# A gated delta net with an FP4 feed-forward layer on one core: every engine meets the steps of an element in another order

## The reference

```python
xn = layernorm(x)
x = x + delta_net(xn) + fp4_ffn(xn)

# delta_net: 12 heads, keys of 64, values of 128
q, k, v = (silu(causal_conv4(xn @ W)) for W in (Wq, Wk, Wv))
q, k = l2norm(q) * 64 ** -0.5, l2norm(k)
g, beta = -exp(A_log) * softplus(xn @ Wgk + dt_bias), sigmoid(xn @ Wb + b_b)
for t in range(256):                       # per head, S is 64 x 128
    S = S * exp(g[t])
    S = S + outer(k[t], (v[t] - k[t] @ S) * beta[t])
    o[t] = q[t] @ S
o = o * rsqrt(mean(o * o) + 1e-5) * g_norm_weight * silu(xn @ Wg)
out = o @ Wo

# fp4_ffn: inputs, weights and the 352 hidden values are rounded
# to FP4 in blocks of 16 along the last axis
h = silu(quant(xn) @ quant(w_gate).T) * (quant(xn) @ quant(w_up).T)
out = quant(h) @ quant(w_down).T
```

## Time and profile before

| | |
|---|---|
| median of 3 runs | 2864.97 us |
| lowest, highest | 2863.22, 2868.68 us |
| the profiled execution | 2873.21 us |
| its span | 2871.5 us |
| instructions | 73819 |
| mean granted clock of TensorE | 0.984 |
| busy: PE, DVE, ACT, POOL | 92%, 84%, 80%, 57% |

### The profile page before, as it was taken

How to read it: one execution, slowest core, us unless ns; L and a number is a source line. 1 busy time by engine, 2 the same in 40 slices (tenths; PEclk the granted TensorE clock), 3 DMA queues, 4 the chain that set the end, 5 groups by cost and what they waited for, 6 DMA issues and landing times.

```text
span 2871.5 us, 73819 instructions
## 1 busy us (share of the span) xinstructions
PE 2652.8 (92%) x25679; PEld 2086.6 (73%) x25679; DVE 2419.4 (84%) x6817; ACT 2289.1 (80%) x7010; POOL 1634.4 (57%) x2418
## 2 busy tenths in 40 slices
...
PEclk8899999999999999999999999999999999999997
...
GB/s 69 22 37 20 30 37 33 31 36 16 36 37 32 32 30 21 36 37 30 34 28 24 35 37 26 37 26 24 37 37 26 37 18 32 37 37 26 36 14 24
DMA packets 319326, 90.30 MB, mean 31 GB/s; under 512 B 283056, under 2 KB 310000, under 8 KB 318960
## 3 DMA queue, kind: packets, MB, share of 16 engines
...
...
## 4 chain that ended last, share of the span: by engine, by line
PE 45%; DVE 27%; POOL 13%; issue 6%; DMA 4%; ACT 3%; SPq 2%; DVEq 0%; POOLq 0%; ACTq 0%
DVE UP L982 7%; POOL laneT L587 5%; POOL laneA L590 5%; DVE vc L887 5%; DVE KQ L887 5%; PE bank_o L1308 4%; PE ring L1142 4%; PE ring L1200 4%; PE bank_e L1278 3%; PE ring L1167 3%; PE ring L1343 3%; PE bank_e L1290 3%; PE bank_e L1294 2%; PE bank_e L1285 2%; PE ring L1108 2%
## 5 line engine op out<-in xcount | busy, mean ns | idle before, releaser
L590 POOL TENSOR_TENSOR laneA<-laneA,laneT 96x30 f32<-96x30 f32 (+14 forms) x960 | 513.1, 534 | 75.2
L587 POOL TENSOR_TENSOR laneT<-laneA 96x30 f32<-96x30 f32 (+14 forms) x960 | 516.9, 538 | 68.0
L887 DVE SCALAR_TENSOR_TENSOR KQ<-ring,ckq,KQ 128x255 f32<-128x255 f32 (+2 forms) x1152 | 459.6, 472 | 10.2 <-ACT KQ L672 4.4
L887 DVE SCALAR_TENSOR_TENSOR vc<-ring,cvv,vc 128x255 f32<-128x255 f32 (+2 forms) x1152 | 461.8, 470 | 0.0
L1027 DVE SCALAR_TENSOR_TENSOR V<-bank_o,eG,V 128x128 f32<-128x128 f32 x384 | 133.4, 347 | 284.5 <-PE bank_o L1314 203.1
L982 DVE SCALAR_TENSOR_TENSOR UP<-ring,cj,gm 128x256 f32<-128x256 f32 x768 | 315.4, 476 | 22.4 <-PE ring L1167 19.7
L575 POOL TENSOR_TENSOR sqk<-sse,phalf 128x8 f32<-128x8 f32 x96 | 157.4, 1640 | 250.3 <-DVE sse L957 250.3
L569 POOL TENSOR_TENSOR gm<-g,mle 128x512 f32<-128x512 f32 x192 | 197.5, 1051 | 175.8 <-DVE UP L982 165.7
L751 ACT ACTIVATE eps<-bank_e 128x128 f32<-128x128 f32 x384 | 106.2, 276 | 219.8 <-PE bank_e L1294 182.8
L582 POOL MEMSET laneA<- 96x32 f32 x32 | 4.9, 154 | 473.8 <-DMA laneA<-to_lanes 473.8
L600 POOL TENSOR_TENSOR rO<-ov,mhalf 128x8 f32<-128x8 f32 x96 | 166.4, 1733 | 155.9 <-DVE ov L1038 155.4
...
## 6 DMA issues: line engine op xcount, KB each, us to landing
to_lanes<-UP SPq DMA_DIRECT2D x128, 96.0 KB, 2.7
...
UP<-from_lanes SPq DMA_DIRECT2D x128, 96.0 KB, 3.1
...
xin<-_attn_hidden_states_dram SPq DMA_DIRECT2D x32, 128.0 KB, 3.6
xres<-_attn_hidden_states_dram SPq DMA_DIRECT2D x32, 128.0 KB, 2.2
```

Source lines behind the costliest of these rows:

```text
L587: link(nc.gpsimd.tensor_tensor(t, A[:, 0:m, j:j + 1].broadcast_to([LANES, m, n]), A[:, j:j + 1, j + 1:BLK].broadcast_to([LANES, m, n]), AL ...
L590: link(nc.gpsimd.tensor_tensor(w, w, t, ALU.add))
L887: ins = nc.vector.scalar_tensor_tensor(acc[:, n, s:T], src[:, n * T:n * T + T - s], wt(n)[:, TAPS - 1 - s:TAPS - s], acc[:, n, s:T], ALU.m ...
```

## The change

The table `ORDER` is replaced by another with the same steps. Besides, an unused table `KEEP` and blank lines go, so a line after stands 23 lower than the same line before (L558 becomes L535, L903 L880, L1308 L1285). The count of the instructions of each kind is the same. Some steps change their offset, that is, they go over the iteration's border: `LANEP 6` and `7`, `STORE` and `XR` from 1 to 0 (the same work, done in the next iteration), and `VPs 4` too. Around the places of the next section the diff reads, cut:

```diff
 ORDER = (
-    ("QK", 0, 1), ("VPs", 5, 0), ("ZB", 0, 1), ("QKr", 0, 1), ("ZBr", 0, 1), ("QKt", 0, 1), ("QK", 1, 1),
-    ("QN", 5, 1), ("MZ2r", 0, 0), ("LN", 0, 2), ("SE", 3, 0), ("GRr", 4, 1), ("SSr", 2, 1), ("XQ0", 0, 1),
-    ("FU", 0, 1), ("LOUT", 0, 1), ("SQ", 8, 0), ("FUr", 0, 1), ("SE", 9, 0), ("LLOAD", 0, 1), ("FUm", 0, 1),
+    ("VPs", 4, 0), ("VPs", 5, 0), ("QK", 0, 1), ("ZB", 0, 1), ("ZBr", 0, 1), ("QK", 1, 1), ("QKr", 0, 1),
+    ("VT", 5, 0), ("QKt", 0, 1), ("KW", 0, 0), ("VT", 2, 0), ("QK", 2, 1), ("LANEP", 6, 0), ("ZBe", 0, 1),
+    ("LANEP", 7, 0), ("QK", 3, 1), ("ZBg", 0, 1), ("GC", 0, 1), ("QKr", 1, 1), ("VTr", 2, 0), ("QK", 4, 1),
+    ("SE", 8, 0), ("GRr", 11, 1), ("MZ2r", 2, 0), ("SO", 8, 0), ("LOUT", 0, 1), ("SQ", 8, 0), ("GP", 0, 0),
+    ("LLOAD", 0, 1), ("SE", 9, 0), ("VPt", 3, 1), ("SQ", 9, 0), ("SO", 9, 0), ("FU", 0, 1), ("FUr", 0, 1),
+    ("LN", 0, 2), ("SQ", 10, 0), ("SE", 10, 0), ("SO", 10, 0), ("GPr", 0, 0), ("FUm", 0, 1), ("LANEP", 0, 1),
```

More of the change, by code:

```diff
@@ L25 @@
 TURNED = 3
-KEEP = ((("CJ", 2, 1), ("KTr", 0, 1)), (("CJ", 2, 1), ("OS", 0, 1)), (("KW", 0, 0), ("SO", 5, 0)), (("KW", 1, 0), ("SO", 5, 0)), (("KW", 2, 0), ("SO", 5, 0)), (("KW", 3, 0), ("SO", 5, 0)), (("ZBr", 0, 1), ("XQ0", 0, 1)), (("ZB", 0, 1), ("QK", 2, 1)), (("ZBr", 0, 1), ("QKt", 2, 1)), (("QK", 2, 1), ("FU", 0, 1)), (("GPr", 0, 0), ("OG", 0, 0)), (("GPr", 1, 0), ("OG", 1, 0)), (("GPr", 2, 0), ("OG", 2, 0)), (("GPr", 3, 0), ("OG", 3, 0)), (("GPr", 4, 0), ("OG", 4, 0)), (("GPr", 5, 0), ("OG", 5, 0)))
 WEIGHTS_AT = ("FU", 0)
@@ L73 @@
-    ("CJ", 2, 1), ("GRr", 8, 1), ("VPs", 1, 1), ("GR", 5, 1), ("GRr", 9, 1), ("MX", 2, 0), ("GRr", 10, 1),
-    ("GRr", 11, 1), ("XQ0", 1, 1), ("MZ2r", 1, 0), ("SE", 6, 0), ("SO", 6, 0), ("VP", 3, 1), ("VPr", 3, 1),
-    ("SE", 7, 0), ("SO", 7, 0), ("XQ", 0, 1), ("MY2r", 2, 0), ("XQr", 0, 1), ("SE", 8, 0), ("SO", 8, 0),
-    ("FU", 0, 1), ("LOUT", 0, 1), ("SQ", 8, 0), ("FUr", 0, 1), ("SE", 9, 0), ("LLOAD", 0, 1), ("FUm", 0, 1),
[14 rows of a table removed]
-    ("OTr", 3, 0), ("VPr", 5, 1), ("OT", 5, 0), ("STORE", 0, 1), ("OTr", 4, 0), ("WO", 3, 0), ("VPs", 4, 1),
@@ L92 @@
-    ("WO", 4, 0), ("HQ", 3, 1), ("OTr", 5, 0), ("HT", 0, 1), ("VPt", 5, 1), ("HT", 1, 1), ("HTr", 0, 1),
-    ("WO", 5, 0), ("HTr", 1, 1), ("YOr", 0, 0),
+    ("VPs", 4, 0), ("VPs", 5, 0), ("QK", 0, 1), ("ZB", 0, 1), ("ZBr", 0, 1), ("QK", 1, 1), ("QKr", 0, 1),
+    ("VT", 5, 0), ("QKt", 0, 1), ("KW", 0, 0), ("VT", 2, 0), ("QK", 2, 1), ("LANEP", 6, 0), ("ZBe", 0, 1),
+    ("LANEP", 7, 0), ("QK", 3, 1), ("ZBg", 0, 1), ("GC", 0, 1), ("QKr", 1, 1), ("VTr", 2, 0), ("QK", 4, 1),
+    ("QKr", 2, 1), ("GCr", 0, 1), ("KW", 2, 0), ("STORE", 0, 0), ("QKs", 0, 1), ("QKt", 1, 1), ("VP", 0, 1),
```

13 lines of the change are left out of this document (added), and 37 rows, old and new, of the table ORDER.

## The result

The changed kernel takes 3003.36 us (median of 4 runs, 2996.27 to 3008.48) beside 2866.28 for the kernel before: 1.0477 times as long, 95% interval 1.0453 to 1.0501. The prediction was 3085 with a range of 2945 to 3190. The sign, the place and the two causes came out as forecast; the size was 82 us too high, since two terms of the sum were too large: what the late load of x costs at full clock, and what the clock costs.

The account below looks back on a forecast made before the run. The loop from MZ 0 through twelve matrices, lane DMAs and POOL was taken as the bound, 86.7 us an element. Stall to 89.6 plus clock 4.2 gave 93.8; x 30 = 213, plus 6, made 3085 us, range 2945 to 3190.

Parts of the forecast that it names:

- the two causes: Late load of x behind the lane load, +90 us at full clock; PE clock falls at MZ and SO 11, 4.2 us an element.
- What bounds the kernel: Loop from M (PE begins MZ 0) through DVE's twelve matrices, lane DMAs and POOL back to M: 86.7 us an element.
- The parts that give: PE's waits at L1136 and L1290 go, putting PE 1.7 us ahead; worth nothing, since PE does not set the loop.
- The late matrices and the load of x: Twelfth matrix at M + 24.8 instead of 21.5, x at M + 33.2, DVE stalls 4.8 us; next M at M + 89.6.
- the last one, from OS 2 to the next M: End of the lane chain: 23.0 us from OS 2 to POOL's last copy, then 10.3 for DMAs until M.
- The clock: Falls at MZ in three of four elements, 4 us each, and at SO 11 in half, 2.4 each: 4.2 an element.
- the page's PEclk: Sign: 7 to 9 in most slices if right; 9 throughout with L880 waiting means only the clock part falls, near 2955.
- The sum: 93.8 - 86.7 = 7.1 us an element, x 30 = 213, + 3 start, + 3 next to last element: +219, 3085 us.
- Stall without clock loss: Rival: the wait for x as worked out, clock staying at 1.00; +90, 2955 us; chance 0.18.
- More clock loss: Rival: a fall at both MZ and SO 11 in every element, 5 + 3.4 us; 3210 us; chance 0.10.
- No change: Rival: stall and gains cancel, or the late load hides behind waits DVE had in the scan anyway; chance 0.03.
- faster: Rival: PE sets the period, so its removed waits count, at most 3.0 us x 31 = 93; 2772 us; chance 0.05.

Follow-up runs that it names:

- a3: Changed kernel with x loaded right behind FETCH and QK 5 put back between MY and MZ 0: 2883 us, 1.0054 of the kernel before.
- s1: Changed kernel with LN ahead of FU 0 instead of behind it: 2991 us, 1.0439 of the kernel before.
- a2: Changed kernel with QK 5 put back between MY and MZ 0: 2966 us, 1.0351 of the kernel before.
- a1: Changed kernel with the load of x issued early, right behind FETCH: 2944 us, 1.0266 of the kernel before.
- a4: Changed kernel with the load of x issued between LOUT and LLOAD: 2915 us, 1.0152 of the kernel before.
- b1: Kernel before with LN alone moved behind SO 9, and so behind LLOAD: 2913 us, 1.0157 of the kernel before.

## Why the prediction was right, and where it was off

**What bounds the kernel.** Right. The loop from M through twelve matrices, lanes and POOL back to M is the one in which the time was lost and found.

**The parts that give.** In after nothing was gained, as forecast. Slot 9 ended on DVE at 1974.97 + 0.27, M + 28.4, as predicted, and PE was ready for slot 11 at 1976.29 + 1.35, M + 30.8 (predicted: 31.4, with a wait of 0.4 taken off that is 0.18 in the earlier trace rows). But the other moves are worth something once the load of x and QK 5 are put right: the clean elements of a3 take 85.9 us, those of before 86.7. The forecast had this gain at nothing; which move gives it was not tried.

**The late matrices and the load of x.** For the clean element (M = 1946.80):

| step | predicted | measured |
|---|---|---|
| twelfth matrix done | M + 24.8 | M + 24.4 |
| load of x issued | M + 29.6 | M + 29.1 |
| LN starts | M + 33.2 | M + 32.4 |
| DVE's wait | 4.8 | 4.0 (mean 4.4) |
| LANEP 0 starts | M + 35.3 | M + 34.4 |
| PE's wait at SO 11 | 3.8 | 3.6 (mean 3.9) |
| OS 2 starts | M + 56.3 | M + 56.1 |
| OS 2 to the next M | 33.3 | 31.6 |
| next M | M + 89.6 | M + 87.7 |

The first seven are off by at most 0.9 us. The term of the sum that failed is the last one, from OS 2 to the next M. It was taken from one element of before and is 1.7 us too large: POOL needed 22.2 us from OS 2 to the end of the copy instead of 23.0, and from there to M 9.4 instead of 10.3. Three of POOL's pieces in that element of before took 1.1 to 1.2 us where one of their size takes 0.6; here one did. Of the other 0.9, the store of `yb` may be a part, which in before goes out between the lanes' two stores (the earlier trace rows leave it out) and now 12 us ahead of them (at 2011.4, the lanes at 2023.0); that was not tried by itself. So at full clock the change cost 87.7 - 86.7 = 1.0 us an element and not 2.9, a third of what was forecast; this rests on one clean element (s1 has one of 87.8, a2 two of 88.0 in mean).

**The clock.** Right that it falls, at these two places, and through these two causes: a2 takes the falls at MZ away with QK 5, a1 and a4 those at SO 11 with the wait. The sizes were off. At MZ it fell in 15 of 30 elements, not in three of four, at about 3.3 us each (the twelfth matrix ends at M + 25.9 to 29.1, 27.8 in mean, instead of 24.5; the price of one fall in before, 3.0 in the forecast, is 24.8 - 21.6 = 3.2 by its rows). At SO 11 it fell in 29, not in half, but an element with that fall alone takes about 89.1 us instead of 87.7: 1.4 us, not 2.4. Together 90.8 - 87.7 = 3.1 us instead of 4.2. One sign was badly chosen: the page's PEclk was to show 7 to 9 in most slices, and 9 throughout was to speak against the clock. It is 9 in 35 of 40 slices, where before has 37, with 44 falls in between.

**The sum.** 93.8 predicted, 90.8 measured: 1.9 us from the loop at full clock (1.7 of them the last term) and 1.1 from the clock, x 30 = 90 us too many. The start gave back about 5 of that: the first M came 8.5 us later (131.3 instead of 122.8), and 3 were in the sum. That leaves 85, where the forecast was 82 too high. Of the 130 us between the two profiled executions the clock is about 31 x 3.1 = 96, the rest of the loop 31 x 1.0 = 31. The forecast had the clock at 30 x 4.2 = 126 of 219.

**The rivals.** "Stall without clock loss" has the nearer time (2955 against 3003, the forecast 3085), but its mechanism is not what happened. "More clock loss" wanted a fall at both places in every element, near the upper sizes; it was 15 and 29 of 30, at 3.3 and 1.4 us. "No change" and "faster" fell with the wait of L880. The range of 245 us held both the stall without clock loss and the forecast, so the time alone couldn't tell them apart; the falls in the trace do. That DVE's late LN would be free where x is in time was not among the rivals; b1 shows that it isn't, through the clock.
